# A two-layer decoder on one core: cross attention started on batch 0 alone, with the other batches' norms in its steps, and the head-dim-8 attention carrying the norms of its own sums and the first routing masks

## The reference

```
x = LN(x + conv_attn(x))      # sigmoid(conv) * tanh(conv), a decay scan, a projection, an RMS norm
x = LN(x + cross(ctx, x))     # keys and values of [LN(ctx), LN(x)]: 16 heads of 64, 32 + 512 keys
x = LN(x + ffn(x))            # ffn: self attention, 16 heads of 8, then LN, then routing to 4 experts
```

## Time and profile before

| what | value |
|---|---|
| median of 3 runs (lowest, highest) | 1878.14 us (1878.12, 1881.32) |
| the profiled execution, its own time | 1882.82 us |
| its span, first to last instruction | 1880.9 us |
| mean granted TensorE clock | 0.955 of full speed |
| TensorE busy | 1664.8 us, 89% of the span |
| VectorE busy | 1298.7 us, 69% |
| ScalarE busy | 958.8 us, 51% |
| GpSimd busy | 302.2 us, 16% |
| DMA queues | 44.37 MB at 24 GB/s on average |

### The profile page before, as it was taken

The page is one execution under the profiler, slowest core; times in us unless marked ns, Lnnn a source line. Parts: engine busy times, 40 slices in busy tenths (PEclk is TensorE's granted clock), DMA queues, the critical chain, the costliest instruction groups (busy, mean ns, idle before and its releaser), DMA issues.

```text
span 1880.9 us, 24972 instructions
## 1 busy us (share of the span) xinstructions
PE 1664.8 (89%) x8069; PEld 738.3 (39%) x8074; DVE 1298.7 (69%) x3068; ACT 958.8 (51%) x2064; POOL 302.2 (16%) x465
## 2 busy tenths in 40 slices
PE   6789999999999989999799988444898899999998
PEld 2245545545544432222244331122443355544443
DVE  7477767767767768888476479999666677753333
ACT  2555656556645526666533566333235366664333
POOL 0000000000000121121077300000000222123443
PEclk9999999999999989999999999777799799999999
DMA  4000000000000211240000000000100513000000
GB/s 188 1 1 1 1 1 1 1 1 1 1 1 2 73 39 41 72 114 2 1 0 1 0 1 1 1 1 1 68 0 3 146 52 81 19 2 1 1 0 23
DMA packets 19807, 44.37 MB, mean 24 GB/s; under 512 B 3872, under 2 KB 13024, under 8 KB 18912
## 3 DMA queue, kind: packets, MB, share of 16 engines
q1 hardware_dynamic: 19200, 42.39, 7.6%
q10 hardware_dynamic: 480, 0.39, 0.1%
HBM read 32.74 MB, written 9.44 MB: 22 GB/s over the span
## 4 chain that ended last, share of the span: by engine, by line
PE 73%; DVE 17%; ACT 5%; issue 4%; POOL 0%; DMA 0%; ACTq 0%; POOLq 0%; SPq 0%; DVEq 0%
PE ps L569 8%; PE ps L535 7%; PE ps L547 6%; PE ps L1069 6%; PE ps L1107 5%; PE ps L973 5%; PE ps L504 4%; PE ps L1518 3%; PE ps L1406 3%; PE ps L1519 3%; PE ps L1417 3%; PE ps L1526 2%; DVE arena L1882 2%; PE ps L524 2%; DVE arena L1863 2%
## 5 line engine op out<-in xcount | busy, mean ns | idle before, releaser
L1229 DVE TENSOR_REDUCE stat<-ps 128x1 f32<-128x512 f32 (+3 forms) x512 | 278.4, 581 | 85.4 <-PE ps L973 41.4
L1160 ACT ACTIVATE arena<-ps 128x512 f32<-128x512 f32 (+3 forms) x512 | 246.4, 515 | 149.7 <-PE ps L1107 81.6
L681 ACT ACTIVATE arena<-ps,stat 128x544 f32<-128x544 f32 x256 | 180.4, 710 | 226.0 <-DVE stat L723 226.0
L723 DVE TENSOR_REDUCE stat<-ps 128x1 f32<-128x544 f32 x256 | 173.4, 719 | 145.1 <-PE ps L535 144.2
L1107 PE MATMUL ps<-arena 75*128 75x512 bf16 (+1 forms) x480 | 163.1, 344 | 10.2 <-ACT arena L1160 7.8
L973 PE MATMUL ps<-arena 72*128 72x128 bf16 (+1 forms) x480 | 163.0, 348 | 8.0 <-DVE stat L1229 7.7
L569 PE MATMUL ps<-arena 128*64 128x512 f32 (+1 forms) x640 | 159.9, 611 | 6.3 <-DVE arena L743 5.5
L535 PE MATMUL ps<-arena 64*128 64x272 f32 x1024 | 153.1, 417 | 12.1 <-ACT arena L681 10.4
L689 ACT COPY arena<-ps 128x512 f32<-128x512 f32 x256 | 137.2, 593 | 16.8 <-PE ps L547 16.8
L547 PEld LDWEIGHTS ps<-wA_sb,arena 128*128 128x128 f32 x1024 | 115.1, 142 | 68.8 <-issue 68.0
L547 PE MATMUL ps<-wA_sb,arena 128*128 128x128 f32 x1024 | 139.8, 280 | 0.0
(11 more groups left out here) (372 smaller groups left out, 2816.1 us busy)
## 6 DMA issues: line engine op xcount, KB each, us to landing
arena<-b_parts SPq DMA_DIRECT2D x180, 96.0 KB
b_parts<-arena SPq DMA_DIRECT2D x64, 128.0 KB, 1.8
reg<-wM_dram SPq DMA_DIRECT2D x1, 3072.0 KB, 10.5
reg<-wB_dram SPq DMA_DIRECT2D x1, 2048.0 KB, 11.4
reg<-wM_dram SPq DMA_DIRECT2D x1, 2048.0 KB, 16.1
reg<-wD_dram SPq DMA_DIRECT2D x1, 1817.0 KB, 10.6
wF_sb<-wF_dram SPq DMA_DIRECT2D x1, 1476.0 KB, 19.3
reg<-b_parts SPq DMA_DIRECT2D x12, 96.0 KB
```

Of the source, the lines that this page charges most:

```text
L681: e.activation(prob_of(P, r).rearrange("p (a k) -> p a k", a=2), score_banks(r), ACT.Exp, bias=x_neg[:, at_:at_ + 1], accum_out=x_sums[:, ...
L723: e.tensor_reduce(x_neg[:, n % 4:n % 4 + 1], score_banks(r), AX.XY, ALU.max, negate=True).then_inc(sem("max_done"), 1)
L1160: e.activation(p_t[:, m % 8, q0:T], ps[:, S1 + m % S2, q0:T], ACT.Exp).then_inc(exp_done, 1)
L1229: e.tensor_reduce(nm[:, G % 2, u // 4, u % 4:u % 4 + 1], ps[:, step % S1, 0:keys(u)], AX.X, ALU.max, negate=True).then_inc(max_done, 1)
```

## The change

The start does batch 0's chain of norms alone, with the other work put between its links: the scans and residual sums of batches 1 to 3, and the context's keys and values (`ctx_parts`), whose PSUM banks are now 5 to 7. `y1` now lies in `x_aux`. The first eight value projections move into steps 0 and 1 of the cross attention. The three norms of batches 1 to 3 move into its bank-7 slots, one batch ahead (`chain_at`): "m2" and "ml" are centring matmuls in r = 3 of head pairs 0 and 2, "s1", "s2" and "sl" sums of squares in r = 1 of head pairs 0, 2 and 3. The next batch's value projections leave head pairs 2 and 3 for r = 1 and r = 3 of head pairs 4 to 7. In the head-dim-8 attention the norm of batches 0 to 2 is hosted in its steps (`MEANS`), and so are the first route and the first masks (`ROUTE_AT`); the expert stage starts as soon as the steps are over, and hosts batch 3's output projection and norm.

```diff
+            scan(0)
+            scan(1)
+            total(0)
+            n1.dve_square(e, 0)
             n_ctx.dve_scale(e, 0)
+            scan(2)
+            n1.dve_scale(e, 0)
+            scan(3)
+            n2.dve_square(e, 0)
+            total(1)
+            total(2)
+            n2.dve_scale(e, 0)
+            total(3)
+            n_lat.dve_square(e, 0)
             link(e, e.tensor_copy(wt_bf[:, 0:128], ident))
+            n_lat.dve_scale(e, 0)
...
             norm_act([(n_ctx, 0)])(e)
+            n1.act_root(e, 0)
+            for hp in range(8):
+                ctx_parts["copy_k"](e, hp)
+            ctx_parts["copy_v"](e, 0)
+            n2.act_root(e, 0)
+            for m in (1, 2, 3):
+                ctx_parts["copy_v"](e, m)
+            n_lat.act_root(e, 0)
+            for m in (4, 5, 6, 7):
+                ctx_parts["copy_v"](e, m)
...
-        add_norms(n1, n2, n_lat)
+        first = lambda x, y: [(x[:, 0, :], y[:, 0, :], T, 0)]
+        n1 = make_norm(first(y1, x_aux), counted("b1_y"), gain="norm_w", eps="eps_attn", mean=False, plus=x_cur)
...
-                if b + 1 < B and hp >= 2 and r == 1:
-                    return b + 1, hp - 2
-                if b + 1 < B and hp in (4, 5) and r == 3:
-                    return b + 1, hp + 2
+                if b + 1 < B and hp >= 4 and r % 2:
+                    return b + 1, 2 * (hp - 4) + r // 2
                 return None
+
+            CHAIN_AT = {(0, 1): "s1", (0, 3): "m2", (2, 1): "s2", (2, 3): "ml", (3, 1): "sl"}
...
                 proj("q", 0)
                 proj("k", 0)
+                ctx_v(e, 7)
                 e.wait_ge(sem("ctx_k_read"), 16)
-                e.wait_ge(sem("v_read"), 8)
                 for i in range(XPAIRS + 7):
                     r, n = i % 4, i // 4 + 1
                     if i < XPAIRS:
                         scores(i)
+                    if i < 2:
+                        for j in range(4 * i, 4 * i + 4):
+                            if j >= 3:
+                                e.wait_ge(sem("v_read"), j - 2)
+                            v_proj(0, j, 4 + j % 3)
...
+                    if i and chain_at(i - 1) and chain_at(i - 1)[0][0] == "s":
+                        chain_root(chain_at(i - 1))
+                    if i < 2:
+                        v_first(4 * i)
+                        v_first(4 * i + 1)
                     if i < XPAIRS:
                         exp(i, 0)
                         exp(i, 1)
+                    if i < 2:
+                        v_first(4 * i + 2)
+                        v_first(4 * i + 3)
...
+                def chain_square(kind, b):
+                    n_ = chain_n(kind, b)
...
+                    e.wait_ge(sem("bank7_written"), qk_before[kind, b] + 1)
+                    e.tensor_copy(t_cent, ps[:, 7, :]).then_inc(sem("bank7_read"), 1)
+                    e.wait_ge(sem("bank7_read"), at7[kind, b])
+                    e.tensor_tensor(t_dev, t_cent, t_cent, ALU.mult).then_inc(c_squared, 1)
+
+                def chain_scale(kind, b):
+                    e.wait_ge(c_rooted, chain_n(kind, b) + 1)
+                    if kind == "s2":
+                        o = e.tensor_tensor(x_cur[:, b, :], t_cent, t_dev, ALU.mult)
...
+            ROUTE_AT = 266
...
+            MEANS = {} if early is None else {64 * b + 112 + 6 * j: (kind, b, 0) for b in range(B - 1)
+                                              for j, kind in enumerate(("mean", "var"))}
...
+                    if MEANS.get(step - 1, " ")[0] == "mean":
+                        mean_square(e, MEANS[step - 1][1])
+                    if MEANS.get(step - 2, " ")[0] == "var":
+                        mean_scale(e, MEANS[step - 2][1])
+                    if early is not None and step == ROUTE_AT + 2:
+                        early["masks"](e)
...
                     for i in range(NI + 3):
+                        if b == 0 and i == 2:
+                            route(e, 1)
+                        if b == 0 and i == 9:
+                            early_parts["last_out"](e)
+                        if b == 0 and i in (11, 14):
+                            early_parts["mean_pe"](e, "mean" if i == 11 else "var", B - 1)
...
-                masks(0)
+                masks(e, 1)
+                early_parts["last_total"](e)
+                early_parts["square"](e, B - 1)
+                early_parts["scale"](e, B - 1)
```

318 lines of the change are left out of this document (209 added, 109 removed).

## The result

| | before | after |
|---|---|---|
| median of the runs, on the same chip | 1878.82 us (6 runs) | 1867.20 us (6 runs) |
| ratio, 95% interval | | 0.9919 [0.9899, 0.9938] |
| the profiled execution, its own time | 1882.82 us | 1868.16 us |
| its span | 1880.9 us | 1866.3 us |
| mean granted TensorE clock | 0.955 | 0.955 |

The change makes the kernel faster, by 0.81% as the ratio has it; the two medians of the table lie 11.6 us (0.62%) apart and the two profiled executions 14.7. The forecast was 1872 us, -0.33%; the time lies inside the given range (1863 to 1882), and the gain is about twice the one that was worked out (6.2 us).

A forecast was written before the change was run, and what follows sets the result against it. TensorE was taken to bound the two attention loops, and engine-to-engine chains the start and the border. Terms -2.7 + 9.9 + 0.7 - 14.1 = -6.2 us, from 1878.1, gave 1872 us; range 1863 to 1882.

The forecast's parts named there:

- The start: Before the cross attention: shortening batch 0's engine-to-engine chain brings the first scores from 87.87 to 58.8, -29.1 us.
- the third rival: At the start, fillers queue in front of the chain's links by over 10 us, making the kernel measurably slower; chance 0.15.
- Steps 0 to 3: First steps of the cross attention: hosted value projections and norm work cost +3.3 us (0 to +6).
- The slots: Cross attention: moved value projections, norm matmuls and late VectorE reads of k cost +23.1 us in all.
- The clock at m: Rival in the cross attention: TensorE's clock falls at five m slots, 1.7 us each, leaving 1880, no change; chance 0.20.
- The head-dim-8 attention: Six hosted norm matmuls, mean and var for three batches, cost 1.65 us each, +9.9 (5.2 to 13.2).
- The border: From the attention's last pv to the experts' second batch: 33.8 us instead of 47.9, -14.1.
- the wait of 2.0 behind the second masks: In the expert stage, TensorE waits 2.0 us at batch 3's mean, its residual sum standing behind 16.2 us of masks.
- The first rival: Means and m slots cost little more than TensorE's own time, 11.8 us better, to 1860; under 1865 has chance 0.12.

The follow-up runs named there:

- the start's half: The kernel before with only the changed start and cross attention; head-dim-8 attention and experts as before: 1876.23 us, ratio 0.9967.
- experiment 3: The changed kernel with the context's key and value projections and their copies behind batch 0's chain of norms instead of between its links: 1875.73 us.
- Experiment 4: The changed kernel with batch 0's eight value projections ahead of step 0 instead of in steps 0 and 1: 1874.59 us.
- `tail_only`: The kernel before with only the hosted norms, route and masks in the head-dim-8 attention and the new border to the experts: 1873.23 us, ratio 0.9955.
- experiment 5: The changed kernel with one more VectorE multiply of 0.7 us, its result unused, in front of s1's scale: 1875.55 us.
- experiment 7: The changed kernel with sl's scale on VectorE behind the next step's maxima instead of in front of them: 1865.74 us.
- experiment 8: The changed kernel with s2's scale and the first multiply of the scales of s1 and sl on GpSimd: 1863.08 us.
- experiment 9: The changed kernel with batch 3's output projection, mean and var four places later in the expert stage: 1867.63 us.

## Why the prediction was right, and where its sizes were off

**The reading of the bounds held.** The gain comes from the two stretches in which no engine was full, and the price from the two loops that TensorE bounds. The halves alone showed it: the start's half ends 5.8 us ahead and the tail's half is worth 8.2 (7.9 lost in the attention, 16.1 won at the border), and they add up.

**The start: right, 0.8 us off.** The chain in front of the first scores was as long as worked out, and experiment 3 shows that the fillers stand in its way for 0.5 to 0.8 us (1.3 had been put in for them): the third rival (slower, chance 0.15) is excluded. That the term was off by only 0.8 is partly luck, since in the profiles with this start the first scores come anywhere between 57.8 and 59.8.

**Steps 0 to 3: +2.9 for +3.3, but by another balance.** I let half of the lost clock come back, 1.1; all of it did, about 2.2 by the longer records of that stretch (up to 3.4, if one takes 0.80 over 17.1 us). So the hosted copies and matmuls must have cost about 5.1 instead of 4.4. Experiment 4 showed that the hosting keeps the clock up. The measured +2.9 also depends on the profile that one compares with: `tail_only`, with the start of before, took 19.1 us for these steps at a clock of 0.64, and against that it would be +0.9.

**The slots: +21.1 for +23.1.** The value projections in r = 3 cost 1.34 each as read from the earlier trace rows. The rest were cheaper: s1 with m2 3.17 per batch instead of 3.55, ml 1.63 instead of 1.95, sl 0.55 instead of 0.7. The mis-sized link is the lateness of the read of k: at m2 it comes 1.06 us later than before instead of 1.2, so that the wait is 1.40 instead of 1.65, and at ml 0.27 instead of 0.45, with a wait of 0.62 instead of 0.85. The mechanism, VectorE's read behind a scale, is the one that experiments 5, 7 and 8 turned up and down, at the forecast sizes but for ml in experiment 8.

**The clock at m: a rival rightly kept, and closer than it looked.** At 1.40 it never fell; with 0.7 us more on VectorE it fell at two of three places of one profile.

**The head-dim-8 attention: +7.3 for +9.9,** the largest mis-sizing. A mean and a var cost 2.4 us together, not 3.3. The output projection's four steps, 1.6 dearer than others, had set my value. But TensorE waits there for the transpose that makes the projection's input:

```profile
772.63 1.12 PE L1077 MATMUL ps<-cent,wC_sb 128*128 128x512 f32 x2 [0.75 <-DVE cent L1237]
```

So 0.75 of the 1.6 was a wait of that matmul alone, and the rest is TensorE's own 0.86. A mean has no such wait, and its four steps (771.76 to 775.67) are 0.8 longer than 3.11. The var is followed by waits of 0.20 and 0.36 for ScalarE's exponentials, and the eight steps that hold it (775.67 to 783.65) are 1.6 longer. That these waits come from the root put in front of the exponentials is likely and was not isolated.

**The border: -16.1 for -14.1.** The term that failed is the wait of 2.0 behind the second masks. TensorE's own 31.8 was right to 0.1 us. The masks began when I said (2.8 us behind the last pv), but I took their length of 16.2 from the earlier trace rows and they took 13.4. Had they taken 16.2 from where they began, TensorE would have waited about 1.7 us for the sum, by an estimate from these rows (sum ready at 17.0 + 2.8 behind the last pv, mean issued at 18.1). The row was measured beside a GpSimd that did not pause, and in the new order GpSimd has pauses; experiment 9 shows that a shorter pause makes the masks longer. The rule of the Trainium skill, GPSIMD Engine Reference, section Key points, that GpSimd and VectorE contend for their shared interfaces where VectorE has two SBUF inputs or a two-port mode, agrees with these rows: a multiplication of two inputs took 1.63 instead of 0.70. The same four one-input instructions took 1.43 us without GpSimd and 2.50 to 5.59 beside it; whether they work in a two-port mode no row says. PSUM reads were left alone in experiment 8. The error was to carry the contended price to a place with another load on GpSimd.

**Together.** 0.8 + 0.4 + 2.0 + 2.7 + 2.0 = 7.9 us, which is -14.1 against -6.2. The sum was off by more than its own size, 14.1 for 6.2, although no term was off by more than 2.6 us. Two of the larger errors are of one kind: the prices of the means and of the masks came from rows that held a wait or a contention which the new places have not. The slots' 2.0 are the lateness of the read of k, taken too long. That all of them lean the same way is not explained further. The profiled execution was forecast at 1876.6 and took 1868.2; that the median lies inside the range is the merit of the range, not of the sum. The first rival ("the slots are cheaper") happened by less than half, 4.6 of its 11.8 us; the border did the rest.

## What to carry to other kernels

A stretch in which the chain hops from engine to engine paid for its shortening in full, and fillers that stood between its links cost 0.5 to 0.8 us there instead of 7.7 behind it. Work that fills waits also kept TensorE's clock up, in steps 0 to 3 above all. Work put into a loop that one engine bounds costs that engine's time plus the lateness of the reads that it waits for, so put the read that frees a shared bank ahead of the long instructions of its engine: that, with some multiplications moved to GpSimd, gained 15 us more here. Before a price is taken from a row, look whether the row holds a wait or a busy neighbour that the new place will not have, since where a sum is a small difference of large terms such errors are as large as the sum.

## What the runs showed of the hardware

The same wait of TensorE, 2.1 to 2.2 us in the same code, is followed by a fall of the granted clock at one time and not at another, 18 of 33 times at the three places above, and the fall (to 0.78 or 0.79 over the step) costs 1.2 to 1.6 us. What decides between the two is open. No fall followed the waits of 1.40 us, nor that of 1.82. Waits of 2.3 us at the start of the cross attention were followed by a fall in all three profiles that have them, to 0.80, 0.81 and 0.64 over steps 0 to 3. Four VectorE instructions from SBUF to SBUF took 2.50, 3.58 or 5.59 us with GpSimd's pauses of 1.17, about 0.4 and none, and 1.43 without GpSimd, while a VectorE read from PSUM beside a GpSimd multiplication kept its 0.68.
